# Rows of q and k stored by place, the down product at the head of a slot, and a diffusion with one matrix for all batches

## The reference, cut to what matters

```
x += zX*(x[d-1] - 2x + x[d+1]) + zY*(x[s-1] - 2x + x[s+1]) + zR*x*(1-x)   # L0, reflect padding
x += (1-sg)*sum_e p_e*expert_e(x) + sg*shared(x)   # L1, 8 experts + 1: silu(h Wg)*(h Wu) @ Wd, F = 512
x += (x A^T) B^T * scaling + embedding             # L2, A and B of the batch's language, rank 16
x += attention(q from side, keys x and own, mask, softmax) @ Wo + bo      # L3, 16 heads of 8
```

## Time and profile before

| | us | share of the span |
|---|---|---|
| median of 3 runs | 469.47 (469.02 to 472.84) | |
| the profiled execution | 469.79 | |
| its span, first to last instruction | 468.0 | |
| PE, matmuls | 422.5 | 90% |
| PEld, weight loads beside them | 330.2 | 71% |
| DVE | 331.0 | 71% |
| ACT | 263.4 | 56% |
| POOL | 175.4 | 37% |

### The profile page before, as it was taken

The page is one execution under the profiler, slowest core; times in us unless marked ns, Lnnn a source line. Parts: engine busy times, 40 slices in busy tenths (PEclk is TensorE's granted clock), DMA queues, the critical chain, the costliest instruction groups (busy, mean ns, idle before and its releaser), DMA issues.

```text
span 468.0 us, 7124 instructions
## 1 busy us (share of the span) xinstructions
PE 422.5 (90%) x2310; PEld 330.2 (71%) x2310; DVE 331.0 (71%) x577; ACT 263.4 (56%) x485; POOL 175.4 (37%) x221
## 2 busy tenths in 40 slices
PE   5898699999999999999999999999987988287795
PEld 2776588786788877878888788787866856165573
DVE  5378967567796879777969886766874856156664
ACT  2476576665556546556465556555542576245672
POOL 3477655659321234233323322222634350011110
PEclk9699999999999999999999999999997999769998
DMA  5333234300012430000233200012763223244510
GB/s 161 90 91 100 81 91 143 99 7 0 23 59 63 127 100 24 4 1 24 72 112 95 69 1 25 1 30 77 205 195 100 73 69 96 72 142 134 152 43 24
DMA packets 50752, 35.98 MB, mean 77 GB/s; under 512 B 4728, under 2 KB 45212, under 8 KB 50716
## 3 DMA queue, kind: packets, MB, share of 16 engines
q1 hardware_dynamic: 50284, 35.44, 25.9%
q10 hardware_dynamic: 432, 0.10, 0.1%
HBM read 25.45 MB, written 10.07 MB: 76 GB/s over the span
## 4 chain that ended last, share of the span: by engine, by line
PE 58%; DMA 12%; DVE 10%; SPq 8%; ACT 5%; issue 4%; POOL 2%; ACTq 0%; DVEq 0%
PE acc_ps L547 5%; PE g_ps L547 5%; PE g_ps L548 5%; PE g_ps L549 5%; PE acc_ps L548 5%; PE acc_ps L549 5%; PE u_ps L549 5%; PE u_ps L547 5%; PE u_ps L548 5%; DMA k_rows<-rows_lo 4%; DVE u_ps L1025 4%; DMA q_pl<-q_rows 3%; SPq L401 3%; DVE act_lo L1029 3%; ACT act_hi L809 3%
## 5 line engine op out<-in xcount | busy, mean ns | idle before, releaser
L809 ACT ACTIVATE act_hi<-u_ps 128x512 fp32r<-128x512 f32 x144 | 86.2, 599 | 101.8 <-DVE u_ps L1025 101.1
L1029 DVE TENSOR_TENSOR act_lo<-u_ps,act_hi 128x512 fp32r<-128x512 f32 x144 | 98.8, 686 | 43.6 <-ACT act_hi L809 41.7
L1025 DVE TENSOR_TENSOR u_ps<-act_p,u_ps 128x512 f32<-128x512 f32 x144 | 99.4, 690 | 22.2 <-ACT act_p L804 17.9
L804 ACT ACTIVATE act_p<-g_ps 128x512 f32<-128x512 f32 x144 | 86.0, 597 | 43.5 <-PE g_ps L549 43.0
L1196 POOL TENSOR_TENSOR xg_lo<-xg,xg_hi 128x512 fp32r<-128x512 f32 x35 | 45.7, 1305 | 136.2 <-ACT xg_hi L815 136.2
L547 PE MATMUL acc_ps<-act_hi,w_split 128*128 128x512 f32 x144 | 61.1, 424 | 3.7 <-DVE act_lo L1029 3.1
L547 PE MATMUL g_ps<-x_hi,w_split 128*128 128x512 f32 x144 | 57.5, 399 | 1.4 <-DVE x_lo L1053 1.4
L548 PE MATMUL g_ps<-x_lo,w_split 128*128 128x512 f32 x144 | 57.1, 396 | 0.0
L547 PE MATMUL u_ps<-xg_hi,w_split 128*128 128x512 f32 x144 | 56.9, 395 | 0.2 <-issue 0.2
L549 PE MATMUL g_ps<-x_hi,w_split 128*128 128x512 f32 x144 | 57.0, 396 | 0.0
L549 PE MATMUL u_ps<-xg_hi,w_split 128*128 128x512 f32 x144 | 56.6, 393 | 0.0
(11 more groups left out here) (154 smaller groups left out, 659.5 us busy)
## 6 DMA issues: line engine op xcount, KB each, us to landing
k_blk<-k_rows SPq DMA_DIRECT2D x64, 48.0 KB
q_pl<-q_rows SPq DMA_DIRECT2D x16, 192.0 KB
q_blocks<-q_rows SPq DMA_DIRECT2D x32, 96.0 KB
k_plain<-k_rows SPq DMA_DIRECT2D x8, 384.0 KB
w_raw<-in_L_cond_Wg SPq DMA_DIRECT2D x8, 256.0 KB, 2.7
w_raw<-in_L_cond_Wu SPq DMA_DIRECT2D x8, 256.0 KB, 2.7
w_raw<-in_L_cond_Wd SPq DMA_DIRECT2D x8, 256.0 KB, 2.9
q_rows<-rows_hi SPq DMA_DIRECT2D x8, 256.0 KB
```

The costliest lines, as they stand in the source:

```text
L804: activation(act_p[m % 2][:], g_ps[m % 2][:], ACT.Silu).then_inc(silu_done, 1)
L809: activation(act_hi[m % 3][:], u_ps[m % 3][:], ACT.Identity).then_inc(act_hi_done, 1)
L1025: tt(u_ps[m % 3][:], act_p[m % 2][:], u_ps[m % 3][:], ALU.mult).then_inc(prod_done, 1)
L1029: tt(act_lo[m % 3][:], u_ps[m % 3][:], act_hi[m % 3][:].bitcast(F32), ALU.subtract).then_inc(act_lo_done, 1)
```

## The change

1. The place becomes the outer part of a row's number in q_rows and k_rows, (s, r, j) in place of (j, s, r), with the weights' columns ordered to suit. The store of a place has 128 rows as its outermost count; the loads of blocks take every fourth row. The copies of the high part are stored once ACT has rounded, ahead of DVE's low part.
2. `load_keys` is split in `load_queries` (mask and q) and `load_blocks`; in the tail the queries of batches 12 and 13 are loaded ahead of pair 3. `place_max` copies the late maxima straight from max_rows to q_blocks.
3. LAG is 3 and the down product stands at the head of the slot.
4. The late scores stand half an iteration later, the late turns at b = 7, 9, 11 and 13 in a part of tp_ps, with a wait of PE for ACT's copy ahead of the projection.
5. The diffusion: ACT makes x_x = zX*x with padded edges in five steps and z_own - zR*x in four; DVE has three operations of two tiles each; POOL makes x_y = zY*x in one operation, and PE uses lap_t for all batches. WARM_PRODUCTS is 8.

The tail waits for values after the first iteration's small steps, not ahead of them. The diff, cut:

```diff
-WARM_PRODUCTS = 4
+WARM_PRODUCTS = 8
-LAG = 2
+LAG = 3
-LATE_SCORES = {(4 + 2 * n + i // 2, i % 2): (B - TB + n, i) for n in range(TB) for i in range(GI)}
-LATE_TURN = {6 + 2 * n: B - TB + n for n in range(TB)}
+LATE_SCORES = {divmod(9 + n * GI + i, 2): (B - TB + n, i) for n in range(TB) for i in range(GI)}
+LATE_TURN = {7 + 2 * n: B - TB + n for n in range(TB)}
...
-            def store_rows(dst, f, places):
-                of_place = dst.rearrange("(j s r) i n -> j s (r i) n", j=GJ, s=3)
-                tok = slice(f * N, f * N + N)
+            def store_rows(dst, f, places, n_rounded, n_drained):
+                tok, rows = slice(f * N, f * N + N), DH * GJ
                 his, lo = places
+                sp.wait_ge(aux_rounded, n_rounded)
                 for s in his:
-                    sp.dma_start(of_place[:, s, :, tok], rows_hi[:].bitcast(F32)).then_inc(rows_stored, 16)
+                    sp.dma_start(dst[s * rows:(s + 1) * rows, :, tok].rearrange("q i n -> (q i) n"), rows_hi[:].bitcast(F32))\
+                        .then_inc(rows_stored, 16)
+                sp.wait_ge(aux_drained, n_drained)
...
+            def load_blocks(b):
+                n, tok = b % 2, slice(b * S, b * S + S)
+                sp.wait_ge(rows_stored, rows_count("key", b // TB))
+                for j in range(GJ):
+                    sp.dma_start(k_blk[n][j:ROW_MASK:GJ, :, j].bitcast(F32), k_rows[j:ROW_MASK:GJ, :, tok])\
+                        .then_inc(keys_loaded[n], 16)
...
-                    sp.dma_start(q_blocks[n][r, :, j].bitcast(F32), q_rows[r, :, tok]).then_inc(pair_loaded[n], 16)
+                    sp.dma_start(q_blocks[n][j:ROW_MASK:GJ, :, j].bitcast(F32), q_rows[j:ROW_MASK:GJ, :, tok])\
+                        .then_inc(pair_loaded[n], 16)
...
-            def load_late_max(b):
+            def place_max(b):
                 n, half = b // PAIR % PBUF, slice(b % PAIR * S, (b % PAIR + 1) * S)
-                sp.wait_ge(max_stored[b % 2], 16 * (b // 2 + 1))
+                sp.wait_ge(max_copied, b + 1)
                 sp.dma_start(q_blocks[n][ROW_MAX:ROW_MAX + 2, :, :, half].rearrange("p i j n -> p (i j) n").bitcast(F32),
-                             max_d[:, :, b * S:b * S + S]).then_inc(late_max[b - (B - TB)], 16)
+                             max_rows[b % 2][:]).then_inc(late_max[b - (B - TB)], 16)
...
             done = TB * (NT - 1)
+            load_queries(done)
+            load_queries(done + 1)
             load_pair(3)
             load_maxima(3)
             stores_of("key", NT - 1, 0)
-            load_keys(done)
-            load_keys(done + 1)
+            load_blocks(done)
+            load_blocks(done + 1)
...
             for t in range(NT):
                 for k in range(SLOTS):
+                    if t * SLOTS + k >= LAG:
+                        down_product(t * SLOTS + k - LAG)
                     if t or k > 1:
                         gate_product(t, k)
                     up_product(t, k)
...
-                    if t * SLOTS + k >= LAG:
-                        down_product(t * SLOTS + k - LAG)
                     scored = score_at(t, k)
...
-                if place == 1 and b in LATE_TURN:
-                    late = LATE_TURN[b]
-                    turn_max(late, min(late + 1, B - 1) * GI + (1 if late + 1 < B else GI), aux_ps)
                 if (b, place) in LATE_SCORES:
                     scores(*LATE_SCORES[b, place], aux_ps)
+                if place == 0 and b in LATE_TURN:
+                    pe.wait_ge(attn_done, b - 1)
+                    turn_max(LATE_TURN[b], 0, tp_ps[b % 2][:, 2 * D:3 * D])
...
+                if b in LATE_TURN:
+                    pe.wait_ge(max_copied, LATE_TURN[b] + 1)
                 if b >= 2:
                     project(b - 2)
...
-            def square(f):
+            def scale_x(f):
...
+                for b in range(TB):
+                    activation(x_x[:, b, 1:D + 1], x_in[:, b], ACT.Identity, scale=z_all[:, 0, TB * f + b:TB * f + b + 1])\
+                        .then_inc(x_scaled, 1)
+                act.wait_ge(x_scaled, TB * f + TB)
+                activation(x_x[:, :, 0:D + 2:D + 1], x_x[:, :, 2:D:D - 3], ACT.Identity).then_inc(x_padded, 1)
+            def weigh_x(f):
...
+                    activation(dif_b[:, b], x_in[:, b], ACT.Identity, scale=z_less[:, n], bias=z_own[:, n]).then_inc(x_weighted, 1)
...
+                    tt(dif_a[:], x_x[:, :, 0:D], x_x[:, :, 2:D + 2], ALU.add).then_inc(dif_step, 1)
                 elif part == 1:
+                    dve.wait_ge(x_weighted, TB * f + TB)
+                    tt(dif_b[:], dif_b[:], x_in[:], ALU.mult).then_inc(dif_step, 1)
                 else:
...
+                    tt(dif_a[:], dif_a[:], dif_b[:], ALU.add).then_inc(dif_ready, 1)
...
+            def scale_y(f):
...
+                tt(x_y[:], x_in[:], over_s(z_all[:, 1, TB * f:TB * f + TB]), ALU.mult).then_inc(y_ready, 1)
```

More of the change, by code:

```diff
@@ L184, in build @@
         v_stage = sb("v_stage", [128, TB, H, VW])
-        mix = sb("mix", [128, TB, S])
+        x_y = sb("x_y", [128, TB, D])
         dif_a = sb("dif_a", [128, TB, D])
@@ L556, in diffuse @@
                     mm(dst, dif_a[:, b], ident, start=True, stop=False)
-                    last = mm(dst, x_in[:, b], mix[:, b], start=False, stop=True)
+                    last = mm(dst, x_y[:, b], lap_t, start=False, stop=True)
                 last.then_inc(aux_written, 1)
@@ L616, in turn_max @@
                 pe.wait_ge(max_split, b + 1)
-                pe.wait_ge(max_done, done)
+                wait(pe, max_done, done)
                 turn(bank[0:2 * H, 0:S], neg_split[b % 2][:].rearrange("p c h -> p (c h)"), ident).then_inc(max_turned, 1)
@@ L815, in round_xg @@
                 activation(xg_hi[n % 2][:], flat(xg), ACT.Identity).then_inc(xg_rounded, 1)
-            def square(f):
+            def scale_x(f):
                 act.wait_ge(x_loaded, 16 * (f + 1))
-                if f:
-                    act.wait_ge(dif_ready, f)
-                activation(dif_b[:], x_in[:], ACT.Square).then_inc(squared, 1)
+                if f == 1:
+                    act.wait_ge(aux_drained, NTH["bias", 0, 0] + 1)
+                elif f:
+                    act.wait_ge(prod_made, TB * (f - 1))
+                    for stored in self_stored:
+                        act.wait_ge(stored, 16 * TB * (f - 1) // 2)
+                for b in range(TB):
[4 more added lines that the diff above has]
+            def weigh_x(f):
+                act.wait_ge(z_ready, 2)
+                wait(act, dif_ready, f)
+                for b in range(TB):
+                    n = slice(TB * f + b, TB * f + b + 1)
+                    activation(dif_b[:, b], x_in[:, b], ACT.Identity, scale=z_less[:, n], bias=z_own[:, n]).then_inc(x_weighted, 1)
             def copy_max(b, bank):
                 act.wait_ge(max_turned, b + 1)
-                wait(act, max_stored[b % 2], 16 * (b // 2))
+                if b - 2 < B - TB:
+                    wait(act, max_stored[b % 2], 16 * (b // 2))
+                else:
+                    act.wait_ge(late_max[b - 2 - (B - TB)], 16)
                 activation(max_rows[b % 2][:], bank[0:2 * H, 0:S], ACT.Identity).then_inc(max_copied, 1)
-            square(0)
+            act.wait_ge(z_loaded, 16)
+            scale_x(0)
+            weigh_x(0)
             split_part(0)
@@ L859, in _ @@
                         round_projections()
+                    for kind, f, b in after_slot(t, k, 5):
+                        if kind == "diffuse":
+                            scale_x(f)
                     for kind, f, b in after_slot(t, k, 4):
                         if kind == "diffuse":
-                            square(f)
+                            weigh_x(f)
             round_act(SLOTS * NT - 1)
@@ L884, in late_work @@
                     aux_step(LATE_FINISH[b, place], NT - 1, 0)
-                if place == 1 and b in LATE_TURN:
-                    copy_max(LATE_TURN[b], aux_ps)
-                    exp_self(LATE_TURN[b], LATE_TURN[b] + 1)
             act.wait_ge(down_done, SLOTS * NT - FC)
@@ L1075, in _ @@
                     m = t * SLOTS + k
-                    if t and k == LAG:
+                    if t and k == LAG - 1:
                         add_experts(t - 1)
@@ L1097, in _ @@
                         small_work()
-                    for part in range(4):
-                        for kind, f, b in after_slot(t, k, 4 - part):
+                    for part in range(3):
+                        for kind, f, b in after_slot(t, k, 3 - part):
                             if kind == "diffuse":
@@ L1214, in split_max @@
                 tt(part[:, 1], neg_all[n][:], part[:, 0], ALU.subtract).then_inc(max_split, 1)
-            pool.wait_ge(squares_loaded, 16)
             pool.wait_ge(z_loaded, 16)
-            for part in range(3):
-                make_mix(0, part)
+            scale_y(0)
             split_part(0)
@@ L1240, in _ @@
```

(7 more changed lines are left out.)

106 lines of the change are left out of this document (42 added, 64 removed).

## The result

The changed kernel took 448.22 us (median of 4 runs, 446.8 to 449.85) against 469.25 before (median of 4): a ratio of 0.954, with a 95% interval from 0.948 to 0.960. The profiled execution took 448.04 us with a span of 446.3. The forecast was 448.6.

The account below looks back on a forecast made before the run. PE was taken as the bound, busy nine tenths of the span, with gains only where it stands still; -3.3 - 2.3 + 4.3 - 7.4 - 12.5 = -21.2 from 469.79 gave 448.6 us, range 440 to 459.

Parts of the forecast that it names:

- start: Kernel start: eight warm products raise PE's clock and the diffusion is written at 13.2 instead of 15.44; -3.3 us.
- diffusion: First group, a little in two later ones: three DVE operations instead of five shorten PE's waits; -2.3 us.
- score ahead of the down product: At nine turns the score must wait for ACT's copy, no longer covered by the down product; 0.48 us each, +4.3.
- rows and loads, in the slots: Last group: faster row stores remove PE's 5.0 us wait for keys and the half-rate clock behind it; -7.4 us.
- tail: After the last store: it lands sooner, batch 12's 10.34 us wait goes, SP's issues then set the pace; -12.5 us.
- early bound of 11.3: Start: the earliest time for PE's eight warm products to end, between 11.3 and 14.6; the forecast took 11.3.
- rival B: Small parts give nothing: warm passes stay slow, ACT's extra steps come through; -13.6 us in all, 456.2, chance 0.08.
- it costs PE 2.5 us directly: First group's diffusion: PE's wait read as the length of DVE's work, so fewer DVE operations would shorten it; 2.5 us.
- Rival C: The score stalls at the other 39 of 48 scores too, for DVE's maximum, at most 0.66 us each; 474.3, chance 0.03.
- SP would be late next: Tail: with batch 12's wait gone, SP's issues delay batch 14's score by 24.5 us from landing; PE waits some 3.
- Rival A: Row stores still take 10 us because memory, not the number of DMA engines, limits them; -9.2, 460.6, chance 0.12.
- the terms named for 440: Low end of the forecast's own terms: tail -17, start -3.7, diffusion -4.0, said to reach 440 us.

Follow-up runs that it names:

- s2: Changed kernel with the old diffusion and four warm products, so with the start of before: 450.75 us, ratio 0.961.
- e3: Changed kernel with the slot's old order (LAG 2, down product ahead of the score): 442.38 us, ratio 0.942.
- after: The changed kernel itself, with the whole change against the kernel before: 448.22 us; its profiled execution took 448.04 us.
- e5: Changed kernel with four warm products, as before, instead of eight: 448.76 us, ratio 0.955.
- e8: Changed kernel with the diffusion of before (five DVE operations, POOL's mix) but still eight warm products: 449.93 us, ratio 0.960.
- e4: Changed kernel with ACT's and DVE's parts of the next group's diffusion one slot earlier: 445.27 us, ratio 0.947.
- e2: Kernel before with only the new row numbering and its loads of every fourth row: 453.7 us, ratio 0.966.
- e1: Changed kernel with the old row numbering, so a store's destination has 4 outermost: 460.61 us, ratio 0.980.
- c4: Changed kernel with the old slot order, diffusion parts a slot earlier, and pairs 5 to 7 loaded by POOL behind its maxima split: 435.44 us, ratio 0.927.
- e7: Changed kernel with the queries of batches 12 and 13 loaded after the last store again: 448.26 us, ratio 0.954.
- c2: Changed kernel with the old slot order and the diffusion parts one slot earlier: 438.99 us, ratio 0.936.

## Why the prediction was right, and where it was not

| term | forecast | measured in the traces |
|---|---|---|
| start | -3.3 | -3.4 (slot 0,2; some -2.2 by all executions, see s2) |
| diffusion | -2.3 | +1.5 in the first group, -0.8 in the next two |
| score ahead of the down product | +4.3 | +5.9 (e3 against after) |
| rows and loads, in the slots | -7.4 | -11.4 (what is left to -8.18 at the last slot) |
| tail | -12.5 | -13.5 (89.7 to 76.2) |
| sum | -21.2 | -21.7 |

- **Start.** The end was right: the diffusion was done at 13.2, as forecast. Inside it two errors met: the products ended at 10.44, earlier than even the early bound of 11.3, and DVE was ready only at 11.1 and not at 9.8, so PE waited 0.73. The slow passes of rival B did not come. And the working gave the whole gain to the warm products; e5 has the same start without them.
- **Diffusion: the wrong step** is "it costs PE 2.5 us directly ..., since DVE runs the parts between the products' own work". I read the wait as DVE's length. It is a matter of place: DVE's last step is put behind slot 13's own product, and DVE runs behind PE. Five steps or three, it ends 2.5 us after PE is there (e8), and a slot earlier it is in time (e4). The +1.5 in the table is the fall of the clock behind that wait, which the execution of the kernel before did not have; the form itself gave nothing in the first group. The Trainium skill's rule (SBUF — State Buffer, Who interferes with whom) was borne out for the steps themselves: 0.69 us with POOL idle, 1.68 and 1.55 with POOL at work, but it bore on nothing that PE waited for. Nor did it speak against the new form alone: four of the old form's five steps also read two SBUF tiles.
- **Down product first.** The mechanism and the nine places were right. The size was low: I let the score start 0.04 us after the copy's end, and it took 0.14 (162.42 to 162.56); the rest is that PE is free for the score 0.03 us after a turn's start (165.79 to 165.82 in the kernel before), and I took 0.14. Together 5.9/9 = 0.66 a turn was lost and not 0.48. Rival C, a stall at every score, did not come.
- **Rows in the slots.** The last group's wait gave 7.5 us (e2: -4.61 to -12.11) against the 7.4 forecast. What the forecast left out is the other 4 us: loads were late in the earlier groups as well. One of them shows in ACT's rows, a weight part in the first group that came 3.13 us late before, 2.71 in e1 and not at all in after and e2. Not all of the 11.4 hangs on the new rows alone. By the same subtraction e1, with the old ones, has some 3 of these 4 us too (1.05 of them at slot 26 of the second group, where a score stood 0.81 before) and 3.3 of the 7.5. So much comes with either the rows or the rest of SP's change; undoing the rows in the changed kernel costs 5.2 us in the slots (-8.18 against -4.57, and the 1.6 of the clock, which did not fall in e1).
- **Tail.** The store's landing, SP's 24.5 us to batch 14's score (22.9 measured, 390.01 to 412.92), PE's wait there (some 3; 2.83), 8.4 to batch 15 (9.5) and 25.8 to the end (23.8) each came within 2 us of the forecast. That SP would be late next was right, and c4 shows what it was still worth. The store took 4.87 and not 3.6.
- **Rival A** fell: 128 rows outermost made three stores land in 4.87 us, 4 in 10.66, in kernels that differ only in the rows' numbering and what goes with it (after and e1). The DMA share of the 16 engines while they land was 0.26 in e1, about the 0.25 that 4 of 16 would give, and 0.58 in the changed kernel (e1 first, columns as in the earlier trace rows). The Trainium skill's rule on the outermost dimension (DMA: Bandwidth & Descriptors, Why a DMA increments its semaphore by 16 and not by 1) names that cause, and these runs agree. Rival A's sum, 460.6, is what e1 took (460.61): stores that stay slow were priced rightly as a whole, though not place by place (2 forecast and 3.3 measured in the last group's wait, 5.9 and 4.3 in the tail).

```profile
388.90:399.60 10.70, 8.12 (x104) 6.51 (x103) 5.95 (x17) 8.10 (x15) 1.67 (x6) 1.00 0.26 85
```

```profile
385.10:390.00 4.90, 4.90 (x60) 4.06 (x59) 3.15 (x8) 3.66 (x8) 0.56 (x2) 1.00 0.58 199
```

- **The range.** Its lower end was added up wrongly: the terms named for 440 give 469.79 - 17 - 3.7 - 4.0 + 4.3 - 7.4 = 442.0.

So two terms were too kind (diffusion by 3.0, half of it the clock; turns by 1.6) and two too careful (rows by 4.0, tail by 1.0). That these cancelled to 0.5 us is luck.

## What to carry to other kernels

When a tile is stored in several pieces, look at the destination's outermost count before its bytes: here 4 instead of 128 cost 16 us of 469 in the kernel before, and 12 in the changed one, in places far from the store, as loads behind it in its queue came late. A wait for a last step is first a question of where the step stands in its engine's order, and only then of how long it takes; move it a slot before making it cheaper. Where a bank serves a producer that another engine must drain, keep work between the two: a reorder that looks free took 0.66 us at each of nine turns.

## What the runs showed of the hardware

- Behind a stand of 2.5 us PE's clock fell in four of nine profiled executions of these kernels and not in the others. The instructions do not decide it: it fell in after and not in e7, which runs the same ones up to the tail. One fall cost 1.6 us. It may be part of why runs of one kernel lie 1 to 3 us apart (after: 446.8 at a mean clock of 0.999, 449.85 at 0.990).
- The slow stores once held the queue that issues them: SP took 3.64 us to issue the two high stores of the last q in the kernel before and 3.81 in e1, but 0.81 in the changed kernel. At the other pairs of high stores it was 1.1 to 1.6 us with the old rows and 0.8 to 1.1 with the new. Of the kernel before, of e1 and of the changed kernel (start, length):

```profile
337.20 3.64 SPq L366 DMA_DIRECT2D q_rows<-rows_hi  x2
```

```profile
331.68 3.81 SPq L367 DMA_DIRECT2D q_rows<-rows_hi  x2
```

```profile
330.54 0.81 SPq L366 DMA_DIRECT2D q_rows<-rows_hi  x2
```

- POOL issued the four block loads of a pair in 2.37 to 2.50 us (c4), where SP took 3.13 to 3.17 for the same four (c2).
